# Cross attention of a perceiver layer: scores of 2048 keys per group in place of 1024, values in a ring of five chunks, new orders of the slots

## What is computed

```python
q = (x @ Wq + bq).reshape(1, B * N, H, hd)
kv = (cond @ Wkv + bkv).reshape(1, -1, 2, H, hd)
k, v = (kv[:, :, 0], kv[:, :, 1])
...
q = _fq_sym(q, axis=-1)
k = _fq_sym(k, axis=-1)
v = _fq_sym(v, axis=2)
attn = jnp.einsum('bhqd,bhkd->bhqk', q, k)
attn = jax.nn.softmax(attn.astype(jnp.float32), axis=-1)
attn = _fq_unsigned(attn, axis=-1)
out = jnp.einsum('bhqk,bhkd->bhqd', attn, v)
```

## Time and profile before

| | us |
|---|---|
| median of 3 runs (579.38 to 580.21) | 579.42 |
| the profiled execution, its own time | 579.99 |
| its span, first to last instruction | 578.2 |
| TensorE busy, share of the span | 92% |
| VectorE busy | 76% |
| ScalarE busy | 63% |
| mean granted TensorE clock | 0.976 |

### The profile page before, as it was taken

The page is one execution under the profiler, slowest core; times in us unless marked ns, Lnnn a source line. Parts: engine busy times, 40 slices in busy tenths (PEclk is TensorE's granted clock), DMA queues, the critical chain, the costliest instruction groups (busy, mean ns, idle before and its releaser), DMA issues. The chain is left out here.

```text
span 578.2 us, 10630 instructions
## 1 busy us (share of the span) xinstructions
PE 531.2 (92%) x4286; PEld 333.2 (58%) x4286; DVE 442.0 (76%) x840; ACT 363.2 (63%) x430; POOL 28.4 (5%) x28
## 2 busy tenths in 40 slices
PE   3999999999899999999998788699999899996997
PEld 2444555553566566665665555488885555562484
DVE  2599999966899989998999798501394788648893
ACT  5624646464699979988998797510254663775442
POOL 0300000000300110020004200000000000000000
PEclk9999999999999999999998798889999999997999
DMA  8723400042445535552556459802956407000000
GB/s 317 270 74 85 133 1 1 0 127 85 137 146 161 169 110 174 168 169 110 167 164 234 157 177 400 351 1 59 279 244 268 183 1 291 1 0 0 2 2 36
DMA packets 20145, 78.84 MB, mean 136 GB/s; under 512 B 2176, under 2 KB 3200, under 8 KB 16896
## 3 DMA queue, kind: packets, MB, share of 16 engines
q1 hardware_dynamic: 20096, 78.16, 39.4%
HBM read 75.27 MB, written 0.79 MB: 132 GB/s over the span
## 5 line engine op out<-in xcount | busy, mean ns | idle before, releaser
L1120 DVE CUSTOM_DVE_ANT_0 arena<-ps,arena 128x1024 f32<-128x1024 f32 x128 | 152.6, 1220 | 15.9 <-issue 7.8
L1504 ACT ACTIVATE arena<-arena,small 128x4096 int16<-128x4096 f32 x32 | 121.5, 3798 | 2.5 <-DVE small L1133 2.4
L598 PE MATMUL ps<-arena 128*128 128x512 f16 x384 | 100.1, 380 | 0.0
L639 PE MATMUL ps<-small,arena 128*128 128x128 bf16 x1024 | 80.6, 223 | 8.1 <-DVE arena L1140 4.8
L564 PE MATMUL ps<-arena 128*128 128x512 f16 x384 | 85.2, 379 | 1.2 <-DVE arena L1051 1.2
L639 PEld LDWEIGHTS ps<-small,arena 128*128 128x128 bf16 x1024 | 60.2, 99 | 17.5 <-issue 6.7
L1511 ACT ACTIVATE arena<-ps 128x512 int32<-128x512 int32 x96 | 56.9, 593 | 20.9 <-PE ps L639 20.4
L813 PE MATMUL ps<-arena 128*128 128x256 f32 (+1 forms) x288 | 67.4, 397 | 0.7 <-ACT arena L1593 0.7
L813 PEld LDWEIGHTS ps<-arena 128*128 128x128 f32 x288 | 55.7, 194 | 11.9 <-issue 3.3
L564 PEld LDWEIGHTS ps<-arena 128*128 128x128 f16 x384 | 37.2, 98 | 43.6 <-issue 1.5
L655 PEld LDWEIGHTS ps<-arena 128*128 128x128 f16 x1024 | 43.0, 97 | 30.1 <-issue 8.2
(11 more groups left out here) (166 smaller groups left out, 711.1 us busy)
## 6 DMA issues: line engine op xcount, KB each, us to landing
arena<-key_scales SPq DMA_DIRECT2D x64, 512.0 KB, 5.8
arena<-in_ctxT SPq DMA_DIRECT2D x8, 1024.0 KB, 6.0
arena<-in_wg SPq DMA_DIRECT2D x4, 1024.0 KB, 8.4
arena<-in_wo SPq DMA_DIRECT2D x2, 2048.0 KB, 11.9
arena<-in_wu SPq DMA_DIRECT2D x4, 1024.0 KB, 6.8
arena<-in_wd SPq DMA_DIRECT2D x4, 1024.0 KB, 5.9
arena<-in_wuq SPq DMA_DIRECT2D x1, 3072.0 KB, 23.2
arena<-in_wkr SPq DMA_DIRECT2D x1, 2048.0 KB, 12.0
```

The costliest lines, as they stand in the source:

```text
L598: last = pe.matmul(ps[:, bank, :], wv16[wpart][:, k, g * P:(g + 1) * P], ctx16[cpart][:, k, tok], start=(k == 0 and i == 0), stop=(k == KC ...
L639: last = pe.transpose(ps[:, bank, :].bitcast(BF16)[:, b * P:(b + 1) * P], p16[u % 2][:, (8 * q + b) * P:(8 * q + b + 1) * P].bitcast(BF16) ...
L1120: dve.tensor_tensor_reduce(sc[:, u % 2, i * SCW:(i + 1) * SCW], ps[:, 2 * (n % 2):2 * (n % 2) + 2, :].rearrange("p a b -> p (a b)"), skb[: ...
L1504: act.activation(p16[u % 2], sc[:, u % 2, :], ACT.Exp, bias=ebias[:, u % 2:u % 2 + 1], scale=sq[:, i:i + 1], accum_out=rsum[:, u:u + 1]).t ...
```

## The change

1. **Scores by halves.** A unit's scores are two groups of four matmuls on all four row groups, 2048 keys, always into banks 0 to 3. `scale_scores` runs twice a unit over 2048 columns; its second pass starts from the first one's maximum, so `score_max` goes. `exp_bias` moves to GpSimd. The ring of scales holds three buffers of 2048.
2. **Values in a ring** of five chunks of 1024, where there was one buffer of four. Some pieces and roundings of the first group move to VectorE. `scale_values` moves from the middle of slot 8g+1 to the end of slot 8g.
3. **New orders**: the first four units are written out by hand, their scores between the pieces of the first values; the first head's first scales have a transfer of their own; slots 4 to 33 have a new order, and the turns' banks are fixed by quarter.

```diff
+SPAN = 2 * SCW
+HALVES = 2
+RING = 3
...
+        def key_half(u, k):
+            return k if u < QT else 1 - k
...
+        def turn_bank(what, n, q):
+            if what == "p":
+                return 4 + q % 2
+            return 4 + (q % 2 if n == 0 else q == 3)
...
             def scores(u, k):
...
-                if n >= 2:
-                    pe.wait_ge(scu, n - 1)
...
+                if n == 0:
+                    pe.wait_ge(kbe, STEPS)
+                    pe.wait_ge(kevac, 2 * STEPS)
+                else:
+                    pe.wait_ge(scu, n)
...
-                for a in range(2):
-                    row = slice(HD * (2 * cp + a), HD * (2 * cp + a + 1))
-                    last = pe.matmul(ps[:, 2 * (n % 2) + a, :], qT4[row, h, t * P:(t + 1) * P],
+                for a in range(4):
+                    row = slice(HD * a, HD * (a + 1))
+                    last = pe.matmul(ps[:, a, :], qT4[row, h, t * P:(t + 1) * P],
...
                 dve.tensor_tensor_reduce(
+                    sc[:, u % 2, i * SPAN:(i + 1) * SPAN],
+                    ps[:, 0:4, :].rearrange("p a b -> p (a b)"),
+                    skb[:, load % RING, :], 1.0, smax[:, u % 2, 0:1] if k else -3.0e38, ALU.mult, ALU.max,
                     smax[:, u % 2, k:k + 1]).then_inc(scu, 1)
```

VectorE's loop, slots 4 to 34:

```diff
+                if now:
                     scale_scores(s, 0)
+                if half == 1:
+                    store_values(group, 2)
+                if late:
+                    store_pT(s - 2, 2)
+                if half == 0:
+                    store_values(group, 0)
+                if piece and half != 0:
+                    max_values(*piece)
                 if now:
                     scale_scores(s, 1)
+                if s % SLOTS == 0 and s // SLOTS < G:
+                    max_values(*value_piece(s))
+                    scale_values(s // SLOTS)
```

TensorE's loop, slots 4 to 33 (`piece` is the piece of this slot, `following` that of the next):

```diff
                 if now:
                     scores(s, 0)
+                if half == 1:
+                    turn_values(group, 2)
+                turn_p(s - 2, 2)
+                if piece:
+                    project_values(*piece, 7, [0, 1] if s == START else [1])
+                values(s - 2, 0)
+                turn_p(s - 2, 3)
+                values(s - 2, 1)
                 if now:
+                    scores(s, 1)
...
+                if piece:
+                    project_values(*piece, 7, [2])
...
+                if half == 0:
+                    turn_values(group, 0)
+                if piece:
+                    project_values(*piece, 7, [3])
...
+                if half != 1:
                     values(s - 2, 2)
                 if prev:
                     turn_p(s - 1, 0)
...
+                if half == 1:
+                    turn_values(group, 3)
+                    values(s - 2, 2)
+                values(s - 2, 3)
                 if prev:
                     turn_p(s - 1, 1)
+                if half == 0:
                     turn_values(group, 1)
+                if following:
+                    project_values(*following, 7, [0])
```

GpSimd:

```diff
+            for u in range(UNITS):
+                group, half = values_turned_in(u)
...
+                if half == 0:
+                    for c in range(NCH):
+                        round_values(group, c)
+                exp_bias(u)
```

More of the change, by code:

```diff
@@ L38 @@
 F16_UNIT = 2.0 ** 24
-RING = 5
+SPAN = 2 * SCW
+HALVES = 2
+RING = 3
 NH, DH, DR = 16, 128, 64
@@ L85, in build @@
         o_oall = place(4 * QT * D)
+        o_v5 = place(4 * SCW)
         o_tail = o_oall - 65536
@@ L577, in turn_keys @@
                 for half in range(2):
+                    if j == STEPS - 1 and half:
+                        free(5)
                     for hh in range(8):
@@ L582, in turn_keys, with turn_first_scales @@
                     last.then_inc(kbt, 1)
+            def turn_first_scales():
+                pe.wait_ge(s_qTe, 4)
+                pe.wait_ge(kscale, STEPS)
+                pe.transpose(ps[0:16, 7, 0:P], skall[:, 0:16], id32[:, :]).then_inc(skft, 1)
+                read[7] = (skfE, 1)
             def turn_scales():
@@ L688, in _, with first_scores @@
-            read[7] = (s_qTe, 4)
+            read[4] = (kbe, 2 * STEPS - 3)
+            read[5] = (kbe, 2 * STEPS - 2)
+            def first_scores():
+                project_values(0, 4, 7, range(KC))
+                scores(0, 0)
+                project_values(0, 5, 5, [0, 1, 2])
+                turn_scales()
+                project_values(0, 5, 5, [3])
+                turn_keys(STEPS - 1)
+                read[4] = (kbe, 2 * STEPS - 1)
+                read[5] = (kbe, 2 * STEPS)
+                project_values(0, 6, 7, range(KC))
+                scores(0, 1)
+                project_values(0, 7, 6, range(KC))
+                project_values(0, 0, 7, [0])
+                scores(1, 0)
+                project_values(0, 0, 7, [1, 2, 3])
+                project_values(0, 1, 6, [0])
+                scores(1, 1)
+                project_values(0, 1, 6, [1, 2])
+                turn_p(0, 0)
+                turn_p(0, 1)
+                project_values(0, 1, 6, [3])
+                scores(2, 0)
+                turn_p(0, 2)
+                project_values(0, 2, 7, [0, 1])
+                turn_p(0, 3)
+                project_values(0, 2, 7, [2])
+                scores(2, 1)
+                project_values(0, 2, 7, [3])
+                project_values(0, 3, 6, range(KC))
+                project_values(1, 0, 7, range(KC))
+                scores(3, 0)
@@ new lines, in first_outputs @@
+            def first_outputs():
+                turn_values(0, 0)
+                turn_values(0, 1)
+                values(0, 0)
+                values(0, 1)
+                turn_values(0, 2)
+                turn_values(0, 3)
+                turn_p(1, 0)
+                values(0, 2)
+                values(0, 3)
+                turn_p(1, 1)
+                project_values(1, 1, 7, [0, 1])
+                turn_p(1, 2)
+                turn_p(1, 3)
+                values(1, 0)
+                values(1, 1)
+                project_values(1, 1, 7, [2, 3])
+                scores(3, 1)
+                values(1, 2)
+                values(1, 3)
+                turn_p(2, 0)
+                turn_p(2, 1)
+                project_values(1, 2, 7, range(KC))
@@ L754, in _ @@
                     project_first((s - FIRST_OUT - 3) // 2, [2])
-                for g, j, bank in steps[1:2] if s == 0 else []:
-                    project_values(g, j, bank, range(KC))
-                for g, j, bank in inline:
-                    project_values(g, j, bank, [1])
-                if late:
-                    values(s - 2, 1)
-                if half == 1:
-                    turn_values(group, 3)
-                if now:
-                    scores(s, 3)
+                if piece:
+                    project_values(*piece, 7, [2])
                 if s in (FIRST_OUT, FIRST_OUT + 1):
@@ L1573, in _ @@
                 if prev:
-                    store_pT(s - 1, 0)
-                if s:
-                    for g, j, bank in steps:
-                        store_projected_values(g, j, bank)
-                if half == 0 and group:
-                    store_values(group, 1)
-                if prev:
                     store_pT(s - 1, 1)
-                if s == 1:
+                if half == 0:
                     store_values(group, 1)
```

415 lines of the change are left out of this document (215 added, 200 removed).

## The result

| | us |
|---|---|
| median after, 4 runs (587.97 to 592.5) | 590.5 |
| median before on the same chip, 4 runs | 579.4 |
| ratio after / before, 95% interval | 1.0193 (1.0161 to 1.0224) |
| forecast | 583.4 (572.5 to 592) |
| profiled execution after, its span | 587.97, 586.2 |

The account below looks back on a forecast made before the run. It took TensorE, VectorE and ScalarE to be in balance. Start -2.0, slots 4 to 23 +6.8 and slot 24 onward -4.8 made 0.0; the clock's +4.0 gave 584.0 profiled, 583.4 median (572.5 to 592).

Parts of the forecast that it names:

- the two stalls: Slot 10: TensorE stands from 0.54 to 2.95 for turn 2's store, later until 9.25 for turn 3's.
- Plain slots, 6.53: Slots without a group change: both score groups share four banks, each waits for the pass before; +0.07 a slot.
- The lower bound of 2.1: VectorE's pass of 2048 columns: at least 2.1 if most of 1.15 were fixed cost; 2.21 taken.
- Rivals 3 and 4: Plain slots: both waits uncovered, 7.2 a slot, 592 (chance 0.11); four row groups not side by side, some 600 (0.03).
- Group changes, 26.4 for three slots: Slots 8, 9 and 10 take 7.2, 7.8 and 11.4, where the old ones took 23.7.
- the second rival: Group changes stall no more than before, as turn 2's store doesn't hold TensorE: 574.0; chance 0.24.
- The clock behind these waits, 1.5 in each of slots 10 and 18: TensorE's clock drops behind the 2.4 wait, costing 1.5 in slots 10 and 18, 1.0 in 26: +4.0.
- Slot 24 to the last exponentials, -4.8, with +1.0 for the clock: Third group change without pieces and slots behind it: 52.4 against 57.2, plus 1.0 for a clock drop in slot 26.
- The start, -2.0: Up to slot 4's first pass: 41 us of TensorE work from 117.0 and 5.4 of waits, pass at 163.5.
- The bounds in the prediction (-6.9 to +2): Range for the start: -6.9 with no wait, +2 with waits twice as long.
- What follows, 0: After the last exponentials at 360.44: the change leaves this part as it is.
- The first rival: The same as the forecast, but the clock holds behind the waits: 579.4; chance 0.20.

Follow-up runs that it names:

- both traces: Two profiled runs of the unaltered changed kernel: the first 587.97 us, the second, taken later, 592.53 us.
- the first trace: The earlier profiled run of the unaltered changed kernel, with the short store of the scales: 587.97 us.
- the combined kernel: Changed kernel with both turns moved, a piece's third quarter before the second scores, start reordered, small scales store, unread matmuls in slot 25: 572.89 us, ratio 0.9905.
- e4: Changed kernel with turn 2 of the values behind the second scores and turn 3 earlier in group changes: 580.21 us, ratio 1.0015 to the kernel before.

## Why the prediction came out as it did

The direction and the two stalls came as forecast. The size failed at two terms of the sum: the clock from slot 24 on, and the start. By the prediction's own steps:

- **Plain slots, 6.53**: right. 6.57 in both traces, with the 0.47 wait ahead of the second scores. Four row groups took 0.39 and a pass of 2048 2.22 (223.69 to the store behind it at 225.91), where 2.21 was taken. (The lower bound of 2.1 doesn't follow from its reason: were most of the 1.15 a cost paid once, a pass of 2048 would take less than 1.73.) Rivals 3 and 4 fall with that. `exp_bias` took 0.27 (0.3 was taken) and is hidden, which the run with the bias on VectorE shows. No pass of a plain slot waited for scales.
- **Group changes, 26.4 for three slots**: right. 7.25, 7.87 and 11.24 make 26.36 where the clock held. The two stalls are where they were put, and the runs that removed them, one by one and together, took 1.9, 1.1 and 3.1 off slot 10 at the same clock. So the second rival (no more stall than before) falls too.
- **The clock behind these waits, 1.5 in each of slots 10 and 18**: right in size, 1.4. It does not fall each time: in the six traces that have this wait unaltered the two slots were at 11.24 to 11.25 three times and at 12.50 to 12.72 nine times. What decides between the two stays open. With that, slots 4 to 23 came out at +8.4 and +9.9 where +9.8 was forecast.
- **Slot 24 to the last exponentials, -4.8, with +1.0 for the clock: here the forecast failed**, by 3.2 in the first trace and 5.1 in the second. What was wrong is the term of the clock. The prediction gave it only to the long wait of slot 26. Without pieces TensorE waits already in slot 25, 1.25 and 0.66, and again in slots 27 and 28, and the clock fell there as well. In the first trace slot 25 took 8.50, where 6.8 was put, slot 26 9.69, where 9.6 was with the clock, and slots 27 to 30 25.05, where 24.1 was; in the second slot 26 took 10.28 and slots 27 to 30 26.34. The work and the waits were sized well: with the clock held by filling, the third change took 22.87 (forecast 22.6; slot 25 7.18), and in the combined kernel, where slots 27 to 30 took 24.37, the whole stretch took 53.28 (forecast 52.4, or 52.5 by its own parts; 0.4 lies in the last term, 6.16 for 5.75). So the clock cost 2.6 to 3.2 over slots 25 and 26 and 0.7 to 2.0 over the four behind, where 1.0 was taken in all. The trace of before had it at that place: its slot 25 fell to 0.50 behind a wait of 1.68, shorter than the 2.4 that the prediction priced, and the earlier trace rows is the next drop after that one.
- **The start, -2.0**: the second miss, in two parts. The sum took the store of the scales at 1.5 from one row, though that row is one execution. It took 2.6 to 3.3 in seven of eight traces of this start, each time with a fetch of instructions beside it. And the start had no term for the clock, which fell in both traces: behind the longer wait in the second (slots 0 and 1 took 19.6, 3.1 more than in the first, of which the store is 1.7), and in slot 3 in the first, 1.2 us. Slot 4's pass came at 164.45 with the short store and at 166.85 with the long one, where 163.5 was forecast. The bounds in the prediction (-6.9 to +2) held both, the value taken did not; by its own 41 us of work and 5.4 of waits they should have been -7.5 and +3.3. The run with the start's order altered shows the path: a store nearly as long (2.91), a wait of 0.64 in place of 2.96, slot 1 at 5.92 in place of 7.47.
- **What follows, 0**: +1.2 and 0.0. In the first trace the first 20 us of the next stage, in which TensorE is busy throughout, ran at 0.88, before at 0.92; by an estimate from these two figures that is 0.8 of it.

Half of the way between the two traces (590.25) the four stretches are off the forecast by +2.1, -0.7, +4.2 and +0.6, 6.2 in all; the rest of the 7.1 to the median is the 0.57 between before's profile and its median, and 0.25.

The first rival (the clock holds, 579.4) is the opposite of what happened: the clock cost more than was taken. Slots 10 and 18 are mended by order alone, and then the kernel is level with before (e4). Slots 4 to 23, where nothing is filled in, take 134.17 in the combined kernel against 137.70 before, with plain slots of 6.36 against 6.46, so here the new parts with mended orders beat the old ones. How much of the 572.89 against 579.4 the parts themselves (four row groups, passes of 2048) are worth is not shown: the kernel before was not given mended orders or filling, and its clock fell in slot 25 too.

## What to carry to other kernels

Where a wait is added to the busiest engine, price the slower clock behind each wait of a stretch, the short ones in stretches with little work too, and not only behind the longest. When two groups of work share a bank or a buffer, look whose store stands between them in another engine's list, and what long instruction stands ahead of it: here moving two stores and two turns was worth 10 us (590.5 to 580.21, with the clock behind the stalls). A transfer's landing time from one execution is one sample; where a chain hangs on it, put both ends into the range, and look in the trace for what else the DMA engines carried at that moment.

## What the runs showed of the hardware

The same wait of 2.35 us on TensorE, in front of the same turn, was followed by the full clock in three cases and by a drop in nine. Matmuls whose result nobody reads, put into the waits, held the clock at 1.00 and were worth 2.6 us in slots 25 and 26 by themselves, against the first trace. A store to DRAM took 1.35 to 2.87 us at 8 KB and 1.54 to 3.3 at 64 KB, in the same place of the program. In all ten traces in which it was long, one packet of 16 KB that fetches instructions was under way beside it, and the store landed 1.04 to 1.08 us after that packet's end.
